# First attention layer of a four-layer graph network: low parts a round later, shared places for kept scores, the weighted sum three rows behind

## The reference

```python
node_att = jax.nn.softmax(x @ node_w, axis=0)
h = x @ edge_w
e = h @ h.T
e = jnp.where(adj > 0, e, NEG_BIG)
edge_att = jax.nn.softmax(e, axis=1)
output = adj * (node_att * edge_att) @ (x @ weight) + bias
```

## Time and profile before

| | |
|---|---|
| median of 3 runs | 807.37 us (804.45 to 808.33) |
| profiled execution | 806.02 us, of it the profiled span 804.2 us |
| TensorE busy | 750.1 us (93%) |
| VectorE busy | 448.4 us (56%) |
| ScalarE busy | 342.3 us (43%) |
| GpSimd busy | 105.6 us (13%) |
| first layer | from 0 to about 222 us of the span |

### The profile page before, as it was taken

How to read it: one execution, slowest core, us unless ns; L and a number is a source line. 1 busy time by engine, 2 the same in 40 slices (tenths; PEclk the granted TensorE clock), 3 DMA queues, 4 the chain that set the end, 5 groups by cost and what they waited for, 6 DMA issues and landing times.

```text
span 804.2 us, 11798 instructions
## 1 busy us (share of the span) xinstructions
PE 750.1 (93%) x4261; PEld 496.7 (62%) x4304; DVE 448.4 (56%) x934; ACT 342.3 (43%) x524; POOL 105.6 (13%) x214
## 2 busy tenths in 40 slices
PE   7898999698899999999979999999999999999897
PEld 6776766465578878787835554665664546465343
DVE  4485778578858798888853375220262311114455
ACT  4677666566486464646531143231361322224000
POOL 1012121111320011101011120000001000000343
PEclk9999999899899999999999999999999999999999
DMA  8957998786658508400020000000000000000011
GB/s 229 184 104 132 157 151 141 141 143 114 125 96 151 103 2 154 70 1 1 1 81 5 0 1 0 1 0 0 0 1 27 1 0 0 0 0 1 21 39 46
DMA packets 114300, 48.71 MB, mean 61 GB/s; under 512 B 103504, under 2 KB 109776, under 8 KB 114256
## 3 DMA queue, kind: packets, MB, share of 16 engines
q1 hardware_dynamic: 110224, 33.44, 20.7%
q0 software_dynamic: 4032, 14.68, 10.9%
HBM read 35.53 MB, written 2.10 MB: 47 GB/s over the span
## 4 chain that ended last, share of the span: by engine, by line
PE 26%; issue 17%; DVE 9%; ACT 2%; POOL 1%; DMA 0%; POOLq 0%; DVEq 0%; ACTq 0%
PE ps L732 11%; PE ps L921 5%; PE ps L864 4%; PE ps L847 3%; PE ps L911 2%; DVE G L1612 1%; PE ps L588 1%; DVE x L1511 1%; DVE stats L1238 1%; DVE es_lo L1226 1%; DVE tm L1431 1%; DMA adjf<-in_L_gnn_W 0%; DVE agg_lo L1419 0%; PE ps L740 0%; DVE y L1633 0%
## 5 line engine op out<-in xcount | busy, mean ns | idle before, releaser
L732 PE MATMUL ps<-adjT,x 128*128 (+1 forms) x737 | 169.2, 379 | 8.5 <-DVE x L1511 4.3
L732 PEld LDWEIGHTS ps<-adjT,x 128*128 128x128 f16 x768 | 71.8, 98 | 89.8 <-issue 5.6
L650 PE MATMUL ps<-sup,turned 128*128 128x512 f16 x256 | 87.9, 392 | 16.7 <-DMA turned<-pl 11.0
L1226 DVE TENSOR_TENSOR hh_lo<-hf,hh_hi 128x512 fp32r<-128x512 f32 x32 | 22.1, 692 | 134.6 <-ACT hf L1162 133.5
L886 PE MATMUL ps<-adjT,G 128*128 x375 | 82.6, 379 | 0.9 <-ACT hf L1162 0.4
L781 PE MATMUL ps<-H_hi,es_hi 128*128 128x258 f32 x256 | 76.6, 299 | 2.2 <-DVE es_lo L1226 1.7
L781 PE MATMUL ps<-H_hi,es_lo 128*128 128x258 f32 x256 | 72.4, 283 | 0.0
L781 PE MATMUL ps<-H_lo,es_hi 128*128 128x258 f32 x256 | 72.4, 283 | 0.0
L652 PE MATMUL ps<-sup,turned 128*128 128x256 f16 x256 | 71.5, 279 | 0.0
L886 PEld LDWEIGHTS ps<-adjT,G 128*128 128x128 f16 x384 | 37.2, 98 | 45.4 <-issue 0.9
L1278 DVE SCALAR_TENSOR_TENSOR pl<-em,ph 128x1024 f16<-128x1024 f32 x32 | 41.2, 1329 | 33.3 <-DMA turned<-pl 26.6
(11 more groups left out here) (214 smaller groups left out, 1472.1 us busy)
## 6 DMA issues: line engine op xcount, KB each, us to landing
adjb<-in_adj POOLq DMA_DIRECT2D x16, 512.0 KB, 6.3
adjf<-in_adj POOLq DMA_DIRECT2D x12, 512.0 KB, 6.4
x<-in_x SPq DMA_DIRECT2D x4, 512.0 KB, 6.1
out<-adjf SPq DMA_DIRECT2D x16, 128.0 KB, 1.7
adjf<-in_L_gnn_W SPq DMA_DIRECT2D x1, 1024.0 KB, 6.1
W1f<-in_L_gnn_W SPq DMA_DIRECT2D x1, 512.0 KB, 3.8
adjf<-in_L_gnn_W SPq DMA_DIRECT2D x1, 512.0 KB, 3.9
we<-in_L_gnn_edge_w SPq DMA_DIRECT2D x1, 256.0 KB, 3.9
```

Of the source, the lines that this page charges most:

```text
L650: ins = mm(bank(6 + u), PT(HI, u)[:, jt, :], sup[:, jt, :], start=(jt == 0), stop=False, skip_group_check=True)
L732: ins = mm(bank(4 + f), x16[:, part, jt, f * P:(f + 1) * P], adj(b, jt), start=(jt == 0 and part == HI), stop=(jt == T - 1 and part == LO))
L1226: return tt(to, frm, high.bitcast(F32), ALU.subtract)
```

## The change

It touches the first layer only.

- **Low parts a round later.** VectorE's round becomes `maxima(t)`, `p_low(t - 1)`, `final0`, `conv_first`, `normed`, with `p_low(15)` behind the loop. ScalarE's `p_high(t)` now waits for each half of `p_low(t - 1)`.
- **Weighted sum three rows behind.** `SUMMED` gives `weighted(0)` in round 2, none in round 3, and `weighted(t - 3)` from round 4 on; `final0` of that row comes one round after. The turned rows have a third place (`turned_2`), and `turn_p(t)` waits for `weighted(t - 3)`. Behind the loop stand `weighted(13)`, two `turn16`, `weighted(14)`, `project16(0)`, `weighted(15)`.
- **All rows' scores kept.** `MIRROR` goes: rows 0 and 1 are kept too, outside their own first bank, and every mirrored tile is transposed from `kept`. `kept` shrinks to 75 places that are given out anew when a row's use ends. Row 0 is first put into `em[:, 1]` and copied into place by `place_row0` (1536 columns), since its place is still in use by `x @ weight`.
- **Order.** ScalarE's round is `keep_row(t)`, `make_fill(t + 1)`, `exp_row(t)`, `p_high(t)`, conversions. `weighted(0)` waits for `sup_lo` piece by piece. SyncE waits for all weighted sums before it turns row 8 of the second layer. Pieces of the conversions for the second layer move between rounds.

```diff
+    PLACES = 75
+    SUMMED = {t: t - 2 if t < TB - 1 else t - 3 for t in range(2, T) if t != TB - 1}
+    HIGH_ROUND = {T - 4: range(0, 2), T - 3: range(2, 6), T - 2: range(6, 10)}
+    LOW_ROUND = {T - 2: range(0, 4), T - 1: range(4, 9)}
+    def kept_banks(t):
+        return range(max(TB, t + 1) // TB, B) if t < T - 1 else ()
...
-        def PT(part, u):
-            return turned[:, 2 * u + part, :, :]
+        def PT(part, t):
+            return turned_2[:, part, :, :] if t % 3 == 2 else turned[:, t % 3 * 2 + part, :, :]
...
                 sp.wait_ge((p_hi, p_lo)[part], 2 * t + 2)
-                wait_from(sp, pv_mm, t - 1)
+                wait_from(sp, pv_mm, t - 2)
...
+                if t == 2 * TB:
+                    sp.wait_ge(pv_mm, T)
...
-                    for m in range(max(MIRROR, TB * c), min(own, TB * c + TB)):
+                    for m in range(TB * c, min(own, TB * c + TB)):
...
-                weighted(t - 2)
+                if t in SUMMED:
+                    weighted(SUMMED[t])
...
-            weighted(T - 2)
+            weighted(T - 3)
             turn16(0)
             turn16(1)
+            weighted(T - 2)
             project16(0)
             weighted(T - 1)
...
+            def place_row0():
+                act.wait_ge(s_kept, banks_kept(1, -1))
+                act.wait_ge(p0_mm, P0_GROUPS)
+                run(kept[:, 0:T - TB, :]..., em[:, 1, CB:N], ACT.Copy).then_inc(row0_placed, 1)
...
             def p_high(t):
                 wait_from(act, PT_landed[HI], 16 * t)
                 act.wait_ge(exp_done, t + 1)
                 for h in range(2):
+                    if t:
+                        act.wait_ge(p_lo, 2 * t - 1 + h)
...
-                keep_row(t)
+                if t > 2:
+                    keep_row(t)
+                if t + 1 < T:
+                    make_fill(t + 1)
                 exp_row(t)
                 p_high(t)
-                if t + 2 < T:
-                    make_fill(t + 2)
+                conv_high(HIGH_ROUND.get(t, ()))
...
-                maxima(t, u, CONV_ROUND.get(t, ((), ()))[0])
-                if t >= 3:
-                    final0(t - 3, 1 - u)
-                conv_first(CONV_ROUND.get(t, ((), ()))[1])
-                p_low(t, u)
-                if t >= 3:
-                    normed(t - 3, 1 - u, x[:, t - 3, :])
+                maxima(t, u)
+                p_low(t - 1, 1 - u)
+                m = SUMMED.get(t - 1)
+                if m is not None:
+                    final0(m, m % 2)
+                conv_first(LOW_ROUND.get(t, ()))
+                if m is not None:
+                    normed(m, m % 2, x[:, m, :])
...
-            conv_first(range(10, 12))
+            p_low(T - 1, 1)
+            conv_first(range(9, 11))
+            final0(T - 4, 0)
+            conv_first(range(11, 12))
+            normed(T - 4, 0, x[:, T - 4, :])
             final0(T - 3, 1)
```

More of the change, by code:

```diff
@@ L117, in build, with banks_kept, kept_places, kept_at @@
     assert HID == CB and N == 2 * 8 * P
+    def kept_banks(t):
+        return range(max(TB, t + 1) // TB, B) if t < T - 1 else ()
+    def banks_kept(t, last):
+        return sum(len(kept_banks(r)) for r in range(t)) + sum(c <= last for c in kept_banks(t))
+    def kept_places():
+        until, first_at = [0] * PLACES, {}
+        for r in range(T - 1):
+            for c in kept_banks(r):
+                tiles = range(max(TB * c, r + 1), TB * c + TB)
+                at = next(s for s in range(PLACES) if len(until[s:s + len(tiles)]) == len(tiles)
+                          and all(last <= r for last in until[s:s + len(tiles)]))
+                until[at:at + len(tiles)] = tiles
+                first_at[r, c] = at
+        return first_at
+    KEPT_FIRST = kept_places()
+    assert [KEPT_FIRST[0, c] for c in range(1, B)] == [TB * c - TB for c in range(1, B)]
+    def kept_at(t, c):
+        return KEPT_FIRST[t, c // TB] + c - max(c // TB * TB, t + 1)
     def w_tiles(w):
@@ L144, in build @@
         sb(before, "first_block_2", [P, T, CB], BF16)
-        kept = sb(before, "kept", [P, sum(T - 1 - t for t in range(MIRROR, T - 1)), P])
+        kept = sb(before, "kept", [P, PLACES, P])
+        turned_2 = sb(before, "turned_2", [P, 2, T, P], F16)
         before.close()
@@ L625, in scores @@
                 wait_from(pe, s_kept, banks_kept(t, -1))
+                if t == TB:
+                    pe.wait_ge(row0_placed, 1)
                 for c in range(B):
@@ L628, in scores @@
                         wait_from(pe, e_read, 2 * (t - 1) + c // 2 + 1)
-                    for m in range(max(MIRROR, TB * c), min(own, TB * c + TB)):
+                    for m in range(TB * c, min(own, TB * c + TB)):
                         ins = nc.tensor.transpose(ps[:, c, (m - TB * c) * P:(m - TB * c + 1) * P],
                                                   kept[:, kept_at(m, t), :], ident[:, :])
[L632 to L640, removed]
+                    first, last = max(own, TB * c), TB * c + TB
+                    for k in range(KD) if first < last else ():
+                        for p, q in ((HI, HI), (HI, LO), (LO, HI)):
+                            ins = mm(ps[:, c, (first - TB * c) * P:CB],
+                                     hT[p][:, k, t * P:(t + 1) * P], hT[q][:, k, first * P:last * P],
+                                     start=(k == 0 and (p, q) == (HI, HI)), stop=(k == KD - 1 and p == LO))
                     ins.then_inc(e_mm, 1)
@@ L649, in weighted @@
                 for jt in range(T):
-                    ins = mm(bank(6 + u), PT(HI, u)[:, jt, :], sup[:, jt, :], start=(jt == 0), stop=False,
+                    if t == 0 and jt % TB == 0:
+                        pe.wait_ge(sup_lo, jt // TB + 1)
+                    ins = mm(bank(6 + u), PT(HI, t)[:, jt, :], sup[:, jt, :], start=(jt == 0), stop=False,
                              skip_group_check=True)
-                    ins = mm(bank(6 + u, D), PT(LO, u)[:, jt, :], sup[:, jt, 0:D], start=False, stop=(jt == T - 1),
+                    ins = mm(bank(6 + u, D), PT(LO, t)[:, jt, :], sup[:, jt, 0:D], start=False, stop=(jt == T - 1),
                              skip_group_check=True)
@@ L979, in _ @@
             make_fill(0)
+            keep_row(0)
             for n in range(P0_SUP, P0_SUP + 2):
@@ L988, in _ @@
                 group0(n)
+            place_row0()
             act.wait_ge(node_neg, 1)
             run(nl[:, :], nl[:, :], ACT.Exp, bias=nst[:, 2:3], accum_out=nst[:, 3:4]).then_inc(node_exp, 1)
+            keep_row(1)
             act.wait_ge(scale_ready, 1)
@@ L1004, in _ @@
             exp_row(1)
+            keep_row(2)
             p_high(1)
-            make_fill(3)
             for t in range(2, T):
-                keep_row(t)
+                if t > 2:
+                    keep_row(t)
+                if t + 1 < T:
+                    make_fill(t + 1)
                 exp_row(t)
                 p_high(t)
-                if t + 2 < T:
-                    make_fill(t + 2)
[L1013 to L1017, removed]
+                conv_high(HIGH_ROUND.get(t, ()))
+            conv_high(range(10, 13))
             def turned_read(g):
@@ L1294, in final0, with maxima @@
                 moments(u)
-            def maxima(t, u, between=()):
+            def maxima(t, u):
                 dve.wait_ge(fill_ready, t + 1)
+                if t == 1:
+                    dve.wait_ge(row0_placed, 1)
                 masked_max(t, u, 0)
-                conv_first(between)
                 masked_max(t, u, 1)
```

24 lines of the change are left out of this document (8 added, 16 removed).

## The result

The changed kernel takes 797.63 us (median of 4 runs, 796.99 to 799.96) against 806.79 us (804.45 to 808.33) for the kernel before on the same chip: a ratio of 0.9897, 95% interval 0.9858 to 0.9936. The profiled execution took 798.13 us, its span 796.3. The forecast was 798.5.

The account below looks back on a forecast made before the run. VectorE and TensorE were taken as nearly even in an undisturbed round (9.03 us), with VectorE waiting for low turns beside loads. 16.0 us gained by round 15, 8.5 given back: -7.5 from 806.0, so 798.5 us, range 792 to 806.

Parts of the forecast that it names:

- walk: Five engine streams written in order with their waits, times carried forward from 20 us; good to some 3 us.
- The rounds: Up to the end of round 15: 186.4 us, where the trace before has 202.4, so 16.0 us ahead.
- VectorE's round, 8.6: Maxima 2.5, low part 2.3, final 2.4, rstd wait 0.95 and normed 0.4: 8.6 us a round, against 9.03.
- Preface: Before round 4, with added copies of rows 0 and 1: round 3 ends at 72.7, trace 75.4; gain 0 to 3.
- They just clear it: In load rounds the low and high turns run until 8.5 us, the load moves from 8.0 on.
- The double load, 4.8 over the norm: Two loads back to back in round 9 catch the high turn; rounds 11 and 12 lose 4.8 us in all.
- Mirror: In 12 rounds six matmuls become two transposes: 0.5 us a round, 6 us of TensorE's work, nothing by itself.
- The way out, 26.4: From round 15 to the end of weighted(15): 26.4 us, where the trace before has 17.9; 8.5 given back.
- A: Little is left, 803 to 808 us: row 1's high turn falls behind its load, keep_row holds maxima up; chance 0.2.
- B: More is gained, 789 to 794 us: the two back-to-back loads catch nothing, TensorE keeps full clock; chance 0.13.
- C: Slower, 811 to 816 us: each load catches the whole high turn; chance 0.1.
- The rule set aside: DMA engines alternate between queues packet by packet; read as equal time, the two back-to-back loads cost almost nothing: 794.5 us.

Follow-up runs that it names:

- step 4: Changed kernel with GpSimd's bias addition put ahead of its two steps for rstd: 803.54 us, ratio 0.9973.
- step 3: Changed kernel with final0 ahead of the low part: only behind the loop (row 12), 797.17 us; in every round, with waits added, 823.66 us.
- step 1: Changed kernel, one part undone each: sum two rows behind, 807.07 us; low part in its own round, 810.99; rows 0 and 1 computed anew, 796.47.
- step 2: Later load moved from row 5's final to row 8's: in the changed kernel 798.05 us, in the kernel before 803.34 us.

## Why the prediction was right, point by point

- **Total.** -7.5 us were forecast for the end of `weighted(15)`. In the two traces it comes at 220.27 and 213.97, 6.3 us earlier; the path is 8.0 us shorter, since the first `negm` came 1.7 us later in the changed kernel's trace. The other 1.6 of the 7.9 us between the profiled executions are the half clock in the last layer. The forecast also set its walk, 212.8, against the trace, 220.3, though the walk of the kernel before had ended at 218.9: walk against walk it was -6.1. That 798.5 comes so near to 798.13 is in part luck.
- **The rounds.** The walk had the last `negm` 186.4 - 31.8 = 154.6 us after the first; it is 155.2. Rounds 4 to 9 took 56.0 (forecast 56.7), 11 and 12 together 21.9 (22.0), 13 to 15 27.0 (26.3). A plain round was 0.3 us longer than forecast, and shorter rounds among 4 to 7 (round 5: 7.41) made up for it; this part is luck too. Of the waits for low turns the walk left 2 us, and 6.2 came.
- **VectorE's round, 8.6.** It is 8.90. The `rstd` wait of 0.95 was right to 0.01; the term that failed is `normed` 0.4, which is 0.81 beside GpSimd's bias addition. The experiment of step 4 shows it: 0.41 and 8.50. In the kernel before, the low part stood in that place and had this loss: the 2.77 us at 132.52, for 2.36, run beside the bias addition at 132.36. The prediction put them down to ScalarE's `ph`; but with the final first (step 3) a low part at 108.54 took 2.91 us beside GpSimd, with no `ph` running. So the change didn't end the loss, it moved it from `p_low` to `normed`.
- **ScalarE's new wait, 0.** In plain rounds it doesn't appear, as said.
- **Preface.** Forecast 72.7, or 40.9 after the first `negm`; it is 41.4, and 39.9 to 41.4 in the nine other runs with late low parts. The high turn of row 1 stayed ahead of its load.
- **Loads and turns.** "They just clear it" is the step that was wrong in its sizes. The load is issued at 6.4 as forecast, the low turn at 2.5, but the high turn of row 9 at 136.29 - 130.94 = 5.35 and not at 4.3: SyncE's issue of the low turn (2.75 us) stands in front of it. In the other undisturbed rounds that issue takes 1.7 to 2.6 us, and the high turn comes at 4.5 to 5.4. It doesn't clear the load: it lands in 6.3 us at the median, 4.5 without the load. Nobody waited for it in plain rounds, so the sum didn't show it, and step 4 shows how near the edge it was.
- **The double load, 4.8 over the norm.** It is 4.1, but by another victim: the high turn got through with 0.42 us of ScalarE's waiting, and the low turn of row 9 was caught. `maxima(11)` didn't wait, `p_low(10)` waited 3.99 and not 1.5. Right in size, wrong in its path.
- **Mirror.** "Without it TensorE would hold rounds 8 to 11 at 9.2" is wrong: rounds 9 to 11 stay 8.91 with rows 0 and 1 computed anew, and no gain from the kept rows shows.
- **The way out, 26.4.** It is 25.2. The stand before `weighted(13)` was forecast at 3.9 and is 3.86, with the half clock behind it as forecast; but the clock came back within the row, which took 7.05 us and not 9.5. Against that `p_low(15)` waited 1.34 us for its turn, which the walk didn't have. "The third place bears little fruit" holds for the way out alone: in the rounds it is worth the whole gain (step 1).
- **Rivals.** A: no. B's condition (the double load catches nothing) was made in step 2, and its price of 4.8 didn't come, since the collision moved on. C's condition, loads that catch the whole high turn, was made twice. With the early bias (step 4) it held for rows 6 to 8, and its price of 0.9 to 2.5 us a round didn't come: 0 to 0.7. The 6 us lost there are mostly one round of 16.3, in which load and turn were issued 0.1 us apart, a case that no rival named. With the final first (step 3) the turn came later, and 26 us were lost. C had its chance of 0.1 on a margin that was narrower than I had worked out.
- **The rule set aside.** Equal time for both queues gave 794.5; the rows between 142 and 144 us (107 pieces of the load, 9 of the turn) are against it once more.

## What to carry to other kernels

When two streams of DMAs share the engines, look at where in the round each is issued, not only at whether their sum fits: here the same work in the same order took 804 or 794 us by when the loads were issued. Before work is taken away in front of a DMA's issue, ask what that DMA will now meet, and hold it back with a wait on something that happens at the right time. A step made late to hide one wait needs one more buffer behind it, or the next engine inherits the wait.

## What the runs showed of the hardware

**A turn that meets a load, in two ways.** Caught before it has moved, the turn starves while the load goes on at full speed: 107 pieces of q0 and 9 of q1 in 2 us (142 to 144, changed kernel). In one case, a high turn with some 880 of its pieces moved when the load began (kernel with the early bias, 82 us), both nearly stop with busy engines: 17 and 267 pieces (90 to 92), where q1 alone moves 1712 and q0 beside a starved turn 107. By piece, over 16 engines and 2 us: 32 us x 114.6% / 267 = 137 ns against 32 x 110.8% / 1712 = 21 ns. The Trainium skill (DMA: Bandwidth & Descriptors, Queues, rings and completion order) has the engines change between queues packet by packet; the rule doesn't give pieces that are six times as long. Nor is it enough that both queues are under way: between 148 and 150 us of the changed kernel 43 pieces of q0 and 1448 of q1 moved, these in 18 ns each. And between 106 and 108 us of the kernel with the early bias 299 pieces of q1 took 128 ns each with none of q0 among them. What makes them so long stays open.

**VectorE and GpSimd side by side.** `normed` took 0.81 us beside the bias addition and 0.41 without it, and the exchange of two GpSimd instructions removed the difference. VectorE's low part did more to GpSimd: 1.11 us for 0.18 and 1.43 for 0.56 (step 3). In three rounds of that trace the low part waited for a turn and began after the first of the two; they then took 0.18 and 0.56, and where they still overlapped the low part took 2.9 us for 2.36. The runs show that the overlap costs this; that it is the ports isn't shown by them.

**The clock.** The granted clock fell to 0.50 of full speed, 1.2 GHz, with every one of the 22 stands of TensorE between 3.59 and 11.3 us in the first layer of the thirteen traces (from 20 us on). Of 21 stands between 2.3 and 3.5 us, 12 had it and 9 had not, and of eight between 1.9 and 2.2 us two had it; the same stand of 3.45 or 3.46 us before `weighted(13)` had it in two kernels and not in a third (early bias). A forecast for such a stand has to keep both cases.
